# Keys and values of the last stage made for two batches at a time, and the steps around them reordered

## The reference

```python
def L2(x, context):                       # wide: 16 heads of 64
    h = layernorm(x) * gamma + beta
    Q, K, V = h @ Wq, context @ Wk, context @ Wv          # 128 x 1024 each
    p = softmax(Q_h @ K_h.T * 64 ** -0.5)                 # per head, 128 x 128
    return x + (concat(p @ V_h) @ Wo + bo)
def L3(x, context):                       # narrow: 16 heads of 8
    q, k, v = x @ Wq.T, context @ Wk.T, context @ Wv.T    # 128 x 128 each
    p = softmax(q_h @ k_h.T * 8 ** -0.5)
    return x + (concat(p @ v_h) @ Wo.T + bo)
```

## Time and profile before

| | |
|---|---|
| median of 3 runs | 1688.01 us (1687.58 to 1691.29) |
| profiled execution, its own time | 1689.87 us |
| its span | 1688.1 us |
| busy in the span: PE, PEld | 1622.8 us (96%), 1386.1 us (82%) |
| DVE, ACT, POOL | 1172.6 (69%), 1094.0 (65%), 760.0 (45%) us |
| PE's clock, mean over the span | 0.983 of full speed |

### The profile page before, as it was taken

One profiled execution on the slowest core, in us unless ns is written; L12 is line 12 of the kernel. 1 busy time (PEld: TensorE's weight loads), 2 busy tenths in 40 slices (PEclk: granted clock), 3 DMA queues, 4 the chain that ended last, 5 costly groups with the idle time before them and its releaser, 6 DMA issues. The chain is left out here.

```text
span 1688.1 us, 51406 instructions
## 1 busy us (share of the span) xinstructions
PE 1622.8 (96%) x19008; PEld 1386.1 (82%) x19008; DVE 1172.6 (69%) x2330; ACT 1094.0 (65%) x3264; POOL 760.0 (45%) x1126
## 2 busy tenths in 40 slices
PE   7999999999999999979999998979999999999997
PEld 6888888888888888869978887878888888888886
DVE  5777777767777777746757775647777776777762
ACT  5777777767777777733336664456776767777763
POOL 3444444444444444422324442645545454545441
PEclk9999999999999999989999999999999999999997
DMA  7777767778767777630040000015454445444430
GB/s 199 197 187 198 185 188 185 210 204 214 188 189 185 186 197 186 189 110 0 0 113 3 3 3 2 0 38 162 133 154 144 130 137 161 131 129 132 130 106 9
DMA packets 229009, 220.18 MB, mean 130 GB/s; under 512 B 20610, under 2 KB 225092, under 8 KB 228740
## 3 DMA queue, kind: packets, MB, share of 16 engines
q1 hardware_dynamic: 228836, 217.79, 46.8%
HBM read 116.01 MB, written 101.71 MB: 129 GB/s over the span
## 5 line engine op out<-in xcount | busy, mean ns | idle before, releaser
L926 POOL TENSOR_TENSOR L_probs<-L_probs,L_inv_sum 128x1024 f32<-128x1024 f32 x128 | 242.9, 1898 | 87.8 <-DVE L_inv_sum L822 87.8
L710 ACT ACTIVATE L_probs<-L_scores,L_neg_max 128x128 f32<-128x128 f32 x512 | 183.2, 387 | 135.1 <-DVE L_neg_max L802 135.1
L796 DVE TENSOR_REDUCE L_row_max<-L_scores 128x8 f32<-128x1024 f32 x128 | 156.2, 1220 | 43.3 <-PE L_scores L568 43.3
L1930 POOL TENSOR_TENSOR L2L_w_probs<-L2L_w_probs,L2L_w_inv_sum 128x1024 f32<-128x1024 f32 x64 | 121.4, 1897 | 79.1 <-DVE L2L_w_inv_sum L1822 79.1
L828 DVE STREAM_TRANSPOSE L_squares<-L_probs 128x1024 f32<-128x1024 f32 x125 | 153.0, 1224 | 0.3 <-POOL L_probs L926 0.3
L568 PE MATMUL L_scores<-L_kT,L_qT 64*128 64x128 f32 x2048 | 133.3, 280 | 0.9 <-ACT L_kT L699 0.9
L1796 DVE TENSOR_REDUCE L2L_w_row_max<-L2L_scores 128x8 f32<-128x1024 f32 x64 | 78.3, 1223 | 80.3 <-PE L2L_scores L1445 80.3
L619 PE MATMUL L_ring<-L_probsT,L_v 128*64 128x128 f32 x2048 | 126.6, 276 | 5.7 <-issue 2.6
L619 PEld LDWEIGHTS L_ring<-L_probsT,L_v 128*64 128x64 f32 x2048 | 110.5, 137 | 25.7 <-issue 20.4
L568 PEld LDWEIGHTS L_scores<-L_kT,L_qT 64*128 64x128 f32 x2048 | 120.8, 189 | 12.5 <-ACT L_oT L699 8.1
L812 DVE TENSOR_REDUCE L_sums<-L_probs 128x8 f32<-128x1024 f32 x64 | 78.1, 1220 | 65.8 <-ACT L_probs L717 65.8
(11 more groups left out here) (237 smaller groups left out, 4514.6 us busy)
## 6 DMA issues: line engine op xcount, KB each, us to landing
L_relay<-L_squares SPq DMA_DIRECT2D x125, 512.0 KB, 3.4
L_probsT<-L_relay SPq DMA_DIRECT2D x500, 128.0 KB, 3.7
L2L_relay<-L2L_w_squares SPq DMA_DIRECT2D x62, 512.0 KB, 3.2
L2L_w_probsT<-L2L_relay SPq DMA_DIRECT2D x248, 128.0 KB, 2.9
ctx_blocks<-ctx_turned SPq DMA_DIRECT2D x48, 128.0 KB, 3.8
out_x<-x SPq DMA_DIRECT2D x32, 64.0 KB, 2.8
ctx_turned<-ctxT SPq DMA_DIRECT2D x1, 1536.0 KB, 7.1
L0a_wq<-in_L_xattn_Wq SPq DMA_DIRECT2D x2, 256.0 KB, 3.1
```

Source lines behind the costliest of these rows:

```text
L710: done = nc.scalar.activation(slot_probs(at, 0)[:, n, :], scores[:, 0, r, i, :], ACT.Exp, scale=layer_of(at).scale, bias=neg_max[:, n:n + ...
L796: nc.vector.tensor_reduce(row_max[:, s, :], slot(s), AX.X, ALU.max).then_inc(max_ready[s], 1)
L926: nc.gpsimd.tensor_tensor(to, to, inv_sum[:, :, s, :].unsqueeze(3) .to_broadcast([TOKENS, 2, GROUP, TOKENS]), ALU.mult).then_inc(divided, 1)
L1930: nc.gpsimd.tensor_tensor(to, to, w_inv_sum[:, :, s, :].unsqueeze(3) .to_broadcast([TOKENS, 2, GROUP, TOKENS]), ALU.mult).then_inc(w_divid ...
```

## The change

The wide keys are now made only in even steps, for batches t + 2 and t + 3 together, and the wide values only in odd steps, for t and t + 1 together. Both stand at the same place, between the two narrow passes, and fill the same four ring banks, called `w.kv0` to `w.kv3`, each with 512 columns in place of 256. ACT copies three of them out and DVE the second. The two halves of the wide scores follow each other directly. The transpose of the narrow maxima is the last of PE's step instead of standing behind the wide scores, the transpose of the normalised rows stands ahead of the second half of the queries, and DVE, no longer ACT, copies it out. On ACT the second four exponentials come ahead of two copies; on DVE `w_add_up` stands near the start of the next step; POOL's list starts with the narrow operands. The class `Ring` is kept for the earlier stages; `Fills` does the same counting for a list that differs from step to step.

```diff
-    order = [*((f"w.k{g}", 2, "act") for g in CHUNKS_4), ("n.mT", -3, "dve"), ("w.PV0", -1, "act"),
-             ("w.PV1", -1, "act"), ("n.PV", -4, "act"), ("w.q0", 2, "act"), ("n.D", -4, "dve"), ("w.Wo", -1, "dve"),
-             *((f"w.v{g}", 0, "act") for g in CHUNKS_4), ("n.hT", -1, "act"), ("n.oT", -4, "act"),
-             ("w.q1", 2, "act"), ("n.qk", -1, "act"), ("n.v", -3, "act"), ("n.Wo", -4, "dve"), ("w.hT", 3, "act")]
+    order = [("w.PV0", -1, "act"), ("w.PV1", -1, "act"), ("n.PV", -4, "act"), ("w.q0", 2, "act"), ("w.Wo", -1, "dve"),
+             ("n.D", -4, "dve"), ("w.kv0", 0, "act"), ("w.kv1", 0, "dve"), ("w.kv2", 0, "act"), ("w.kv3", 0, "act"),
+             ("n.hT", -1, "act"), ("n.oT", -4, "act"), ("w.hT", 3, "dve"), ("w.q1", 2, "act"), ("n.qk", -1, "act"),
+             ("n.v", -3, "act"), ("n.Wo", -4, "dve"), ("n.mT", -2, "dve")]
...
+    def makes_keys_values(t):
+        return real(t) or real(t + 1) if t % 2 else real(t + 2)
...
+        def keys_or_values(t, g):
+
+            src = bank(f"w.kv{g}", t)
+            if t % 2 == 0:
+                return (w_kT[:, :, :, :].rearrange("p s (c g) t -> p g c s t", g=4)[:, g, :, :, :],
+                        src.rearrange("p (c s t) -> p c s t", c=2, s=2))
...
+            def w_keys(t):
+                ctx_blocks.await_loaded(pe, t + 2)
+                to = [start_fill(f"w.kv{g}", t) for g in QUARTERS]
                 for c in range(2):
                     for r in range(3):
-                        for g in CHUNKS_4:
+                        for g in QUARTERS:
                             part = slice(QUAD * g, QUAD * (g + 1))
-                            last = nc.tensor.matmul(to[g][:, TOKENS * c:TOKENS * (c + 1)], W.wk[part, r, c, :],
-                                                    ctx_blocks.of(b)[part, r, :], start=r == 0, stop=r == 2,
+                            last = nc.tensor.matmul(to[g][:, PAIR * c:PAIR * (c + 1)], W.wk[part, r, c, :],
+                                                    ctx_blocks.pair(t + 2)[part, r, :, :], start=r == 0, stop=r == 2,
                                                     tile_position=(QUAD * g, 0))
...
                 await_emptied(pe, "w.PV0", b)
-                await_emptied(pe, "w.PV1", b)
                 to = start_fill("w.Wo", b)
                 for c in range(chunks):
+                    if c == GROUP:
+                        await_emptied(pe, "w.PV1", b)
...
+            def w_keys_values(t, g):
+                await_filled(dve, f"w.kv{g}", t)
+                nc.vector.tensor_copy(*keys_or_values(t, g)).then_inc(emptied["dve"], 1)
```

More of the change, by code:

```diff
@@ L110, in before, with __init__, count, bank @@
         return engine, (base if at.i is None else at.i * self.per_step[engine] + base)
+class Fills:
+    BANKS = 4
+    def __init__(self, fills):
+        self.nth, self.fill, self.at_fill, self.engine = {}, {}, [], {}
+        seen = {"act": 0, "dve": 0}
+        for name, b, engine in fills:
+            seen[engine] += 1
+            self.engine[name] = engine
+            self.nth[name, b] = seen[engine]
+            self.fill[name, b] = len(self.at_fill)
+            self.at_fill.append((engine, seen[engine]))
+    def count(self, name, b):
+        return self.nth[name, b]
+    def bank(self, name, b):
+        return self.fill[name, b] % self.BANKS
+    def before(self, name, b):
+        n = self.fill[name, b] - self.BANKS
+        return self.at_fill[n] if n >= 0 else None
 def pipeline(engine, step, first, last, steady_first, steady_last, before_loop=lambda: None):
@@ L1304, in wide_and_narrow, with real, keys_made, values_made @@
     LANDED = 16 * SQUARES
-    ring = Ring(order, range(first, last + 1), BATCHES, {LAST_WIDE + 1: turned_by_pe + order})
+    def real(b):
+        return 0 <= b < BATCHES
+    def makes_keys_values(t):
+        return real(t) or real(t + 1) if t % 2 else real(t + 2)
+    def keys_made(b):
+        return b // 2 * 2 - 2
+    def values_made(b):
+        return (b + 1) // 2 * 2 - 1
+    ring = Fills((name, t + lag, engine) for t in range(first, last + 1)
+                 for name, lag, engine in (turned_by_pe if t == LAST_WIDE + 1 else []) + order
+                 if (makes_keys_values(t) if name.startswith("w.kv") else 0 <= t + lag < BATCHES))
     chunks = INNER // 128
@@ L1419, in start_fill @@
             def start_fill(name, b):
[L1420 removed]
+                before = ring.before(name, b)
                 if before:
@@ new lines, in w_values @@
+            def w_values(t):
+                to = [start_fill(f"w.kv{g}", t) for g in QUARTERS]
+                batches = [b for b in (t, t + 1) if real(b)]
+                for b in batches:
+                    for r in range(3):
+                        for g in QUARTERS:
+                            part = slice(QUAD * g, QUAD * (g + 1))
+                            last = nc.tensor.matmul(to[g][:, PAIR * (b % 2):PAIR * (b % 2 + 1)],
+                                                    ctx_blocks.of(b)[part, r, :], W.wv[part, r, :],
+                                                    start=r == 0, stop=r == 2, tile_position=(QUAD * g, 0))
+                            if b == batches[-1] and r == 2:
+                                filled_by(last, f"w.kv{g}")
```

143 lines of the change are left out of this document (66 added, 77 removed).

## The result

The changed kernel takes 1665.76 us, median of 4 runs (1661.72 to 1667.4), against 1687.8 for the kernel before on the same chip (1686.71 to 1691.29): a ratio of 0.986 with a 95% interval of 0.984 to 0.9885, some 22 us. The profiled execution took 1667.4 us, its span is 1665.6. The prediction was 1660, 1644 to 1677.

What follows compares the result with a forecast made beforehand. PE's stream was taken as the joint stage's bound (busy 48.68 of 50 us). Piece changes sum to -1.73 a step, waits add .62 and .06: -1.07, times 26, -28 us from 1688.1, so 1660, range 1644 to 1677.

Steps and rivals of the forecast that it cites:

- Points 1 and 2: PE, each step: keys leave between the wide scores, -1.55 and -.20 us; maxima's transpose no longer stands alone, -.14.
- Point 3: Between PE's narrow passes, 48 records of 256 columns take 2.75 in place of 1.45, +1.30; wider keys save nothing.
- rival (e): A narrow record is mostly a fixed price, so wide keys take 1.55, not 2.75, every second step: 1644; chance .03.
- Points 4 and 5: Second narrow pass finds enough cover, -.44, to .94; the wait ahead of the first pass goes, -.17.
- Point 7: Behind PE's projection near the step's end, a wait of .36 goes and a pause of .34 shrinks to .21: -.43.
- new wait: Ahead of PE's second queries, for ACT's three copies behind the fill: +.62 us a step.
- rival (a): No new wait at the second queries, ACT's copies overlapping the fill: step 15.1, time 1643; chance .12.
- Rival (c): One fill takes all four ring banks; three copies precede the second queries; slower overall at .84 a copy; chance .08.
- rival b: DVE's list becomes the pace, or ACT's copies cost .63: step 16.0 to 16.4, time 1666 to 1677; chance .21.
- (d): Nothing changes: a wait of 1 us for DVE's first maxima, before covered by keys, eats the gain: 1688; chance .06.
- SP paragraph: SP's squares land about 16.5 into the step, wanted at 18.7: slack shrinks from 4.8 to 2.2, nothing waits.
- the ends: Joint stage's start and end: nothing, give or take 3; about +2 to 3 ahead of first scores, step 30 -1.45.

Runs made afterwards that it cites:

- experiment 7: The changed kernel with the maxima's transpose back behind the wide scores and the adding back behind DVE's first subtraction: 1728.63 us, 1.0241 to the kernel before.
- experiment 3: The changed kernel with the same keys made by 128 columns a matmul, 96 records instead of 48: 1669.25 us, 0.989 to the kernel before.
- experiment 4: The changed kernel with ACT copying all four quarters of keys or values, DVE none: 1679.04 us, 0.9951 to the kernel before.
- experiment 5: The changed kernel with two quarters copied by ACT, two by DVE, second queries ahead of normalised rows' transpose, DVE's last maxima ahead of scaling those rows: 1659.85 us.
- experiment 1: The changed kernel with the context's loads spread over four steps, behind the squares' transfers: 1665.25 us, 0.9874 to the kernel before.
- experiment 6: The changed kernel with the edits of experiments 1, 2 and 5 together, DVE's turned squares behind its copies up to step 0 only: 1652.87 us, 0.9777.
- experiment 2: The changed kernel, in its first steps alone: ACT copies first queries ahead of second exponentials, DVE copies keys and normalised rows ahead of turned squares: 1667.03 us.

## Why the prediction was right, and where it was off

**Points 1 and 2** (keys out of the scores, maxima's transpose) are right within .01. That the transpose and its adding move is worth far more than the .14 and .10 given to them (experiment 7). The sum's move to the front of DVE's list probably calls for it; a run with the sum at its old place, which would show that, was not made.

**Point 3** is right in kind and .16 too large: 48 records cost 2.59 to the next start, not 2.75. In the row of 48, without the last one's .38, a record takes .0515 (2.80 - .38, over 47), not the .057 read from the shorter row, and the second pass starts .17 behind the last record's start. That wider keys bring next to nothing is shown by experiment 3, and rival (e) falls. By the Trainium skill, "TensorEngine Tiling (Array Packing)", Instruction Overhead, each matmul costs some 60 cycles; if they came on top of the columns' own time, the 24 more matmuls of experiment 3 would be dearer by an estimated .6 us, or 1.2 if each of the 48 more records counts. The trace has .09, and does not agree with that.

**Points 4 and 5** are right: the second pass falls to 1.00 (.94 predicted), and no wait stands ahead of the first.

**Point 7 and the new wait.** Together they were to leave the end of the step .30 longer; it is .43. The wait for the copies was put at .62 ahead of the second queries. It is .28 there (1327.36 + .11 to 1327.75) and .15 ahead of the transpose before (1327.10 + .11 to 1327.36), .43 in all. ACT's copies behind the fill are these:

```profile
1326.12 1.57 ACT L1724 ACTIVATE L2L_w_kT<-L2L_ring 128x512 f32<-128x512 f32 x3 [1.39 <-PE L2L_ring L1558]
```

They take 1.57 as laid out (2 x .48 + .6), but start 11.73 into the step in place of 12.0, as the fill is shorter, so the second queries start at 13.36 in place of 13.71. In turn the maxima's transpose, now the last of the step, costs .43 to the wide scores here and .34 in other steps, where .21 was taken; why it varies isn't settled. The cause is as predicted: experiment 4 lengthens that wait by one copy, experiment 5, with fewer copies on ACT and another order behind them, takes it away. So rival (a) is not what happened, but a better division of the copies gives a part of it. Rival (c) has its mechanism there, at .48 a copy and not at the .84 that decides. The Trainium skill, "TensorEngine Tiling (Array Packing)", PSUM Bottleneck, asks for both engines on the copies; experiments 4 (+.49 a step) and 5 (-.23) agree.

**The division and the fill (rival b).** DVE's division, the .06 of the sum:

```profile
1322.77 0.29 DVE L1907 TENSOR_TENSOR L2L_n_rows_o<-L2L_ring,L2L_n_inverse 128x128 f32<-128x128 f32 x1
...
1326.17 0.69 DVE L1882 COPY L2L_w_kT<-L2L_ring 128x512 f32<-128x512 f32 x1 [0.19 <-PE L2L_ring L1558]
```

It ends 1323.06, 8.67 into the step (8.8 predicted), and the fill starts at 1323.34 without a wait. DVE's copy takes .69 (.6 taken) and nothing waits for it. (b) did not come about, and neither did (d).

**The SP paragraph failed.** "The slack shrinks from 4.8 to 2.2 and nothing waits" counted the squares' own issues and not the twelve context loads, 6.52 us of SP's queue, that stand ahead of them in steps 8 and 16. With these the squares came back 5.5 us late, which is more than the slack was: 5.3 us in the 26 steps, which experiment 1 gave back.

**The step that failed most is the ends**, "nothing, give or take 3". The end of the stage was -2.3, near what was argued there but within its scatter, and the start +9.2. Only the +2 to 3 ahead of the first scores was seen (it was 2.5). That one fill takes all four banks, and that PE then waits for ACT, was weighed for full steps alone, in rival (c). At the start of the pipeline ACT's list has eight exponentials ahead of the copy, and behind such waits PE had half the clock in places.

In sum: the 26 steps without the late squares would be 407.9, a gain of 30.3 where 28 was predicted; the loads took 5.3 of it, the start 9.2, the end gave 2.3: 18.1 in the joint stage. The other 4.4 of the profiled difference came from the stages ahead, which the change doesn't touch, and that is luck: without them the time would be near 1670, outside the forecast's 1652 to 1666, at a place where rival (b) stood with a mechanism that isn't there. In the full step, too, the fill's -.22 against the sum and the +.13 at its end nearly cancel.

Not settled: the rest of the 9.2 (experiment 6 recovers 4.6, with its first keys at the low clock), and why steps 18 to 21 of the change, or 17 to 19 of experiment 1, take 15.8 to 15.9. At the end of three of them in either run the wide scores wait .2 longer behind the maxima's transpose (.51, 1427.53 to 1428.04 in the change, in place of .34), and the profile names DVE's finish of the narrow rows as what came last.

## What to carry to other kernels

Read a change of a software pipeline in three parts, start, full step and end, and redo the bank and queue argument for each: a plan that is right in the full step lost a third of its gain here (9.2 of 30.3) where half the work is absent. When a step gets shorter, go through every queue for work that comes only every n-th step. Where one fill takes all the banks, what counts is the time from its end to the last copy, so divide the copies over the engines early. Compare profiles stretch by stretch, with the granted clock beside each, before a difference is put down to the code.

## What the runs showed of the hardware

What a wait costs beyond its length differs from run to run. PE's granted clock fell to .50 behind the wait of 3.06 at the start of the stage, and to .56 in the half weighing behind the 2.07 of step 17 (1.75 to the next start, .95 usually). But behind the 2.83 at the start the keys ran at 1.00, and behind step 17's 2.42 in experiment 2 and 2.26 in experiment 5 the half weighing did too (1.02 and 1.03 to the next start). Waits of 1.79 in experiment 7 mostly left the clock at full, yet in its five steps of 19.06 the same wait is followed by queries of 1.39 to 1.67 in place of .96 (.55 behind the one at 1323.44). SP's issues have no fixed price: twelve context loads in a row took 6.52 (.54 each) in step 16, in the kernel before 6.99 and 5.43, three alone 1.25 (.42 each). And a transfer can be slower behind others: the squares' way out took 5.48 to the next issue behind twelve loads, 3.19 without them.
